# One attention layer and a 64-expert layer on one core: the end of the last chunk laid out anew

## What is computed

```python
# attention: 8 heads of 64 features (d = 512 // 64), softmax(q k / sqrt(8)) v
x = layernorm(x + attention(x) @ Wo + bo)
# shared expert, for every token
shared = (silu(g_s) * y_s) @ w_shared_down          # y_s, g_s = split(x @ w_shared_up)
# routed experts: 64 of them, the 6 best of each token, at most 256 tokens for each
scores = sigmoid(x @ w_gate); w, idx = top_k(scores, 6); w = w / w.sum()
pos = running count of the tokens that chose this expert before   # valid if pos < 256
x_disp[e, pos] = x                                   # dispatch
out = (silu(x_disp @ w_up[gate]) * (x_disp @ w_up[value])) @ w_down   # per expert
x = layernorm(x + ... )   # shared + sum over the 6 of w * out, gathered back
```

## Time and profile before

| | us |
|---|---|
| median of 3 runs (lowest to highest) | 1390.62 (1387.7 to 1397.6) |
| the profiled execution, its own time | 1395.11 |
| its span, first to last instruction | 1393.3 |
| PE busy | 1280.9 (92%) |
| DVE busy | 1017.0 (73%) |
| ACT busy | 901.2 (65%) |
| POOL busy | 664.8 (48%) |
| mean granted clock of TensorE, share of full | 0.974 |

### The profile page before, as it was taken

How to read it: one execution, slowest core, us unless ns; L and a number is a source line. 1 busy time by engine, 2 the same in 40 slices (tenths; PEclk the granted TensorE clock), 3 DMA queues, 4 the chain that set the end, 5 groups by cost and what they waited for, 6 DMA issues and landing times.

```text
span 1393.3 us, 24378 instructions
## 1 busy us (share of the span) xinstructions
PE 1280.9 (92%) x8129; PEld 1068.5 (77%) x8129; DVE 1017.0 (73%) x1879; ACT 901.2 (65%) x1639; POOL 664.8 (48%) x662
## 2 busy tenths in 40 slices
PE   6999799999999999999999999996678999999596
PEld 4888599899899899799799799796456767767332
DVE  4623488789799899799799789796445677677376
ACT  5411398878688688688688688686114666666242
POOL 0002122235636636636636636546363888888511
PEclk9999899999999999999999999998798999999899
DMA  6049966112423424324334333334455999997597
GB/s 232 0 186 353 344 215 217 55 37 86 136 70 129 130 86 137 105 86 137 112 95 129 121 102 127 108 107 140 157 204 171 335 353 346 347 359 274 208 419 303
DMA packets 155754, 252.78 MB, mean 181 GB/s; under 512 B 18660, under 2 KB 98916, under 8 KB 153201
## 3 DMA queue, kind: packets, MB, share of 16 engines
q1 hardware_dynamic: 130144, 192.19, 40.9%
q0 software_dynamic: 20992, 50.38, 9.5%
q10 hardware_dynamic: 4496, 8.65, 1.7%
HBM read 118.95 MB, written 134.33 MB: 182 GB/s over the span
## 4 chain that ended last, share of the span: by engine, by line
PE 66%; issue 12%; DMA 6%; SPq 4%; DVE 4%; POOL 4%; ACT 3%; another core or an unknown queue 2%; POOLq 0%; DVEq 0%; ACTq 0%
PE pv_acc L1256 13%; PE slot L1237 13%; PE slot L1224 12%; PE slot L1119 8%; PE slot L1333 4%; PE slot L1283 4%; PE misc L1170 4%; PE pv_acc L1119 4%; DMA got<-y_hbm 3%; SPq L397 3%; DVE rows_lo L1059 2%; ACT rows_hi L783 2%; PE slot L1355 1%; DMA moved<-scaled 1%
## 5 line engine op out<-in xcount | busy, mean ns | idle before, releaser
L740 ACT ACTIVATE p_hi<-slot 128x512 fp32r<-128x512 f32 x512 | 279.8, 596 | 108.6 <-PE slot L1224 86.4
L590 POOL TENSOR_TENSOR p_lo<-prob,p_hi 128x512 fp32r<-128x512 f32 x128 | 165.1, 1290 | 363.4 <-ACT prob L742 356.9
L1237 PE MATMUL slot<-k_stack,q_stack 128*128 128x512 f32 x1024 | 300.8, 416 | 8.5 <-DMA q_stack<-q_hbm 8.5
L753 ACT ACTIVATE prob<-prob,row_min 128x1024 f32<-128x1024 f32 x256 | 296.4, 1158 | 12.9 <-DVE prob L1035 12.9
L1014 DVE TENSOR_TENSOR p_lo<-slot,p_hi 128x512 fp32r<-128x512 f32 x384 | 251.3, 681 | 37.6 <-ACT p_hi L740 31.0
L1256 PE MATMUL pv_acc<-p_hi,v_pair 128*128 128x256 f32 x1024 | 265.6, 292 | 3.9 <-POOL p_lo L590 3.2
L1224 PE MATMUL slot<-ident,prob 128*128 128x128 f32 x2048 | 265.2, 272 | 1.2 <-ACT prob L753 1.2
L1256 PE MATMUL pv_acc<-p_lo,v_pair 128*128 128x256 f32 x1024 | 255.1, 282 | 0.0
L1224 PEld LDWEIGHTS slot<-ident,prob 128*128 128x128 f32 x2048 | 230.8, 140 | 1.7 <-DVE prob L1035 1.6
L1256 PEld LDWEIGHTS pv_acc<-p_hi,v_pair 128*128 128x128 f32 x1024 | 193.0, 189 | 18.0 <-issue 8.6
L1256 PEld LDWEIGHTS pv_acc<-p_lo,v_pair 128*128 128x128 f32 x1024 | 192.8, 188 | 11.7 <-issue 3.3
(11 more groups left out here) (142 smaller groups left out, 2092.4 us busy)
## 6 DMA issues: line engine op xcount, KB each, us to landing
disp_hbm<-zeros SPq DMA_DIRECT2D x64, 512.0 KB, 5.5
rows<-disp_hbm SPq DMA_DIRECT2D x64, 512.0 KB
y_hbm<-zeros SPq DMA_DIRECT2D x48, 512.0 KB
got<-y_hbm SPq DMA_DIRECT2D x16, 1536.0 KB, 11.9
q_stack<-q_hbm SPq DMA_DIRECT2D x128, 128.0 KB
up_w<-in_L_ffn_w_up SPq DMA_DIRECT2D x64, 256.0 KB
down_w<-in_L_ffn_w_down SPq DMA_DIRECT2D x32, 256.0 KB
q_hbm<-q_hi SPq DMA_DIRECT2D x8, 512.0 KB, 2.6
```

What stands on the lines that cost most here:

```text
L590: e.tensor_tensor(p_lo[1][:, 2:4, :], prob[:, m % 2, :, (4 * u + 2) * P:(4 * u + 4) * P], p_hi[1][:, 2:4, :].bitcast(F32), ALU.subtract).t ...
L740: e.activation(p_hi[b][:, two, :], view[:, two, :], ACT.Copy).then_inc(a_phi, 1)
L753: e.activation(keys, keys, ACT.Exp, bias=row_min[:, me % 2, j, 1:2], scale=-1.0, accum_out=row_sum[:, me % 2, j, half:half + 1]).then_inc( ...
L1237: made = e.matmul(slot[:, n * BANK:(n + 1) * BANK], qs[:, part, j * P:(j + 1) * P], k_stack[:, ms % H, keys], start=part == 0, stop=part == 1)
```

## The change

- **Loads within the last chunk.** The rows of items 0 to 6, the residual tiles of the last chunk, the shared weights and seven `up_w` are loaded by SP during the last chunk, each over the keys of a head that is used up (`head_used` waits for that head's last scores). The last chunk's two tiles live in `rows[7]`, which is also item 7: it is not stored and loaded again. The shared weights are split in the attention's drain.
- **Both tiles side by side.** The last chunk's second tile gets its own bank (`pv_acc`), `x1_t`, scores and so on (`routing_of`, `bank_of`).
- **A hand-laid order.** `last_end` replaces `chunk_end` for the last chunk; it starts in the items' loop, and there are three `side_step`s in an iteration: `after(n, part)` names the place after flip (0), up (1) or down (2) of iteration n.
- `P0`, `P1` become 12, 34. The notes of the second tile of chunk 6 wait until attention is over; the scatters of each tile have their own semaphore. The notes of the last chunk come after all its scatters. The table is turned at n = 9, not 7. Weights of experts 0 to 3 are split at n = 0 to 3, not 4 to 7. SP's loads are in a written order.

```diff
-        AHEAD, CLEAR, SIDE, K_ROUTE = NB - 1, NCH - 1, 4, 16
-        P0, P1 = 14, 38
+        AHEAD, K_ROUTE, END = NB - 1, 16, NCH - 1
+        P0, P1 = 12, 34
+        def head_used(e, h):
+            e.wait_ge(p_scores, (END * H + h) * STEPS + STEPS)
+        def rows_of_chunk(c, j):
+            return rows[NS - 1][:, j, :] if c == END else resid[j][:, :]
+        def routing_of(c, j):
+            return routings[1 if c == END and j else 0]
+        def bank_of(c, j):
+            return pv_acc if c == END and j else misc
+        def after(n, part):
+            return 3 * (n + 2) + part
+        def split_at(n):
+            g = n if n < NU else n + NU - NS if n >= NS else -1
+            return range(g, g + 1) if 0 <= g < E else range(0)
...
# SP, called once in each step with s - END * H * STEPS
+            def load_for_shared(s):
+                if s in (6, 10, 14):
+                    for n in (0, 1):
+                        load_rows(e, (s - 6) // 2 + n)
+                elif s == 19:
+                    for j in range(QT):
+                        load_resid(END, j)
+                elif s == 22:
+                    head_used(e, 4)
+                    e.dma_start(sup_w[:, :, :], w_sup[:, :, :]).then_inc(d_sup, 16)
+                    e.dma_start(sdown_w[:, :], w_sdown).then_inc(d_sup, 16)
+                elif s == 28:
+                    load_rows(e, NS - 2)
+                elif s == 33:
+                    for g in range(NB - 1):
+                        load_up(e, g)
...
# SP, after the steps
-            attention_over(e)
-            load_resid(NCH - 1, 1)
...
+            for pair in range(NB // 2):
+                load_down(e, pair)
+            for g in (NB, NB + 1, NB - 1, NB + 2):
+                load_up(e, g)
+            for n in range(NS, NS + NU):
+                load_rows(e, n)
+            load_up(e, NB + 3)
+            for j in range(2):
+                e.wait_ge(d_tabw[j], 16 * TOPK * NCH)
+            e.dma_start(table[:, :], table_hbm.rearrange("(c p) one -> c (p one)", p=P)).then_inc(d_tab, 16)
...
# POOL
                 for k in range(0, TOPK, 2):
-                    yield from to(P1 + 30 + k)
+                    yield from to(P1 + (30 if c < END - 1 else 64) + k)
                     note_rows(2 * c + 1, k)
                     note_rows(2 * c + 1, k + 1)
+            def last_end(c):
+                to = ticks()
+                yield from to(after(-1, 1))
+                root(c, 0)
+                root(c, 1)
+                yield from to(after(1, 0))
+                count(c, 0)
+                for j in range(2):
+                    yield from to(after(1 + j, 2))
+                    e.wait_ge(v_route[j], K_ROUTE * c + 15)
+                    for k in range(TOPK):
+                        scatter(c, j, k)
+                yield from to(after(4, 0))
+                for j in range(2):
+                    for k in range(TOPK):
+                        note_rows(2 * c + j, k)
...
# ACT
+            def last_end(c):
+                to = ticks()
+                yield from to(after(0, 0))
+                flip_x1(c, 0)
+                yield from to(after(0, 1))
+                raise_score(c, 0)
+                flip_x1(c, 1)
+                yield from to(after(0, 2))
+                raise_score(c, 1)
...
# DVE
+            def last_end(c):
+                to = ticks()
+                yield from to(after(-1, 1))
+                add_resid(c, 0)
+                measure(c, 0)
+                add_resid(c, 1)
+                normalize(c, 0)
+                measure(c, 1)
+                yield from to(after(0, 0))
+                normalize(c, 1)
+                for j in range(2):
+                    yield from to(after(0, 1 + j))
+                    for part in (score_experts, choose, mark, mark_any):
+                        part(c, j)
+                yield from to(after(1, 0))
+                for j in range(2):
+                    for part in (sum_top, share, pick_rank, find_place, find_slots, keep_weights):
+                        part(c, j)
+                    yield from to(after(1, 2))
...
# PE
+            def last_end(c):
+                to = ticks()
+                yield from to(after(-1, 1))
+                out_project(c, 0)
+                out_project(c, 1)
+                yield from to(after(0, 0))
+                turn_x1(c, 0)
+                yield from to(after(0, 1))
+                gate_scores(c, 0)
+                turn_x1(c, 1)
+                yield from to(after(0, 2))
+                gate_scores(c, 1)
+                yield from to(after(1, 0))
+                rank(c, 0)
+                yield from to(after(1, 2))
+                rank(c, 1)
```

More of the change, by code:

```diff
@@ L201, in build @@
         d_qst, d_q = [sem(f"dma_q_store{i}") for i in range(2)], [sem(f"dma_q{i}") for i in range(2)]
-        d_moved, d_feats, d_st, d_scat = (sem(f"dma_{n}") for n in ("moved", "feats", "x1_store", "scatter"))
+        d_moved, d_feats, d_st, d_st_late = (sem(f"dma_{n}") for n in ("moved", "feats", "x1_store", "x1_store_late"))
+        d_scat = [sem(f"dma_scatter{j}") for j in range(2)]
         d_resid = [sem(f"dma_resid{j}") for j in range(QT)]
@@ L455, in sync @@
                 side_step(jobs)
-            attention_over(e)
-            load_resid(NCH - 1, 1)
[L459 to L471, removed]
+            for pair in range(NB // 2):
[8 more added lines that the diff above has]
+            e.dma_start(table[:, :], table_hbm.rearrange("(c p) one -> c (p one)", p=P)).then_inc(d_tab, 16)
+            loaded, ups = NS + NU, NB + NU
+            for n in range(NS - 2, NI):
+                while loaded < NI and loaded <= n + (AHEAD if loaded < NS + NB else NB + 1):
+                    load_rows(e, loaded)
+                    loaded += 1
                 for g in range(ups, min(E, n + 4)):
@@ L636, in gpsimd @@
                                 oob_is_err=False).then_inc(d_y[y], 16)
-                for _ in range(SIDE):
-                    side_step(jobs)
+                side_step(jobs)
             def final_root(t):
@@ new lines, in keep_weights, with route @@
+            def keep_weights(c, j):
+                own = routing_of(c, j)
+                e.scalar_tensor_tensor(out=weight_of[:, 2 * c + j, :], in0=own.place[:, :], scalar=float(CAP),
+                                       in1=own.top[:, 0:TOPK], op0=ALU.is_lt, op1=ALU.mult).then_inc(v_route[j], 1)
+            def route(c, j, clock, start):
+                for n, part in enumerate((score_experts, choose, mark, mark_any, sum_top, share, pick_rank,
+                                          find_place, find_slots)):
+                    yield from clock(start + 6 + 2 * n)
+                    part(c, j)
@@ L1284, in tensor @@
                     made.then_inc(p_flip, 1)
-                for _ in range((3 if n == -2 else 1) * SIDE):
-                    side_step(jobs)
+                side_step(jobs)
                 i = n + 1
```

376 lines of the change are left out of this document (195 added, 181 removed).

## The result

The changed kernel is **slower** by 1.7%: 1418.1 us (median of 4 runs, 1412.9 to 1422.9) against 1393.7 (4 runs, the three of the table above and one more, 1387.7 to 1397.6), ratio 1.0166, 95% interval 1.0138 to 1.0194. The forecast was 1358 us. The profiled execution has a span of 1415.0 us (before 1393.3).

The account below looks back on a forecast made before the run. POOL, never idle from first to last `y_hbm` scatter, was taken as the bound, so its first scatter decides: 110.9 us after attention's old end before, 2.8 + 71.3 + 2 = 76.1 after, gain 34.8; forecast 1358 us, range 1349 to 1377.

Parts of the forecast that it names:

- attention, with P0 and P1 earlier and the loads beside it: Attention up to its end: loads hide under full PE and side jobs keep their order; 0, within 2 us.
- The drain: End of attention: four POOL scatters ahead of the last `p_lo` make PE wait, so attention ends 2.8 us later.
- From A' to the first `y_hbm` scatter: From attention's new end to POOL's first `y_hbm` scatter: 71.3 us, plus 2 for the clock.
- The 110.9 us of the kernel before: From attention's last matmul to POOL's first `y_hbm` scatter in the old kernel: the base for the gain.
- From the first scatter to the end: POOL's first `y_hbm` scatter to its last 235.3 us, then 82.5 us to the end: nothing changed.
- Rival 1: Behind attention: ACT's unexplained waits return in POOL's unbroken run; 1376 us with both, 1363 to 1372 with one; chance 0.25.
- Rival 2: Behind attention: notes and table set the end if DVE routes late; `scat` 8 us late gives 1366; chance 0.06.
- Rival 3: Shared stage behind attention: the clock stays at 1.2 GHz, + 48 us, 1408 us; chance 0.04.
- Rival 4: Last chunk: a load over a used key holds SP's queue; 1361 us, whole failure 1385 to 1395; chance 0.03.
- The 0.03 for "slower": Whole kernel: the chance given to a time above the no-change bound of 1404.5 us.

Follow-up runs that it names:

- e6: The changed kernel run once more, nothing altered: median 1399.8 us, ratio 1.0172 to the kernel before.
- e5: The kernel before run once more, nothing altered: median 1378.9 us.
- e2: The kernel before with only P0, P1 = 12, 34 in place of 14, 38: ratio 1.0273 to the kernel before.
- e1: The changed kernel with P0, P1 put back to 14, 38: 1368.4 us, ratio 0.9934 to the kernel before.
- e4: The changed kernel with P0, P1 = 14, 38 and the last chunk's twelve notes left out: 74.7 us from the last head's `scaled` to the first `y_hbm` scatter.
- e11: The changed kernel with P0, P1 = 14, 38, six row loads at s = 7, 11, 15, last chunk's bias additions at 21 and 23: ratio 0.9845 to 0.9882.

## Why the prediction was wrong, point by point

**The step that failed** is the first one: "attention, with P0 and P1 earlier and the loads beside it: 0, within 2 us". On runs without the long waits the attention ends 45.8 us later (959.9 to 1005.7); 4.5 of them are the drain, which had a term of its own, and 41.3 are this step. I argued that PE is full there, that P1 moves by two whole steps and that the side jobs keep their order against `p_lo`. The first two are true, and neither says what a use of `misc` does to the head's own use. The third looked at the order only: with P1 = 34 PE's wait for `p_lo` at a chunk's first head rose from 0.4 to 1.7 us. A stage with PE at 10.00 of 10 us has no slack either: a wait that is put ahead of a `spread` lengthened its head by as much (1.4 us), in each of seven chunks. By the chunks' own lengths, six cost 33.1 us (e6 against e5, 636.3 and 603.2 us from the end of chunk 0 to that of chunk 6), and e2, with nothing but the two numbers changed, 37.6 in all. The remainder is nearly all in the last chunk. Of the loads, the step said that they hide: they do by their volume, but not by their place in the queue (5.5 to 7.5 us in e1; in e6 the head took 18.1 us against 16.9 to 17.1 in the chunks before it, so about 1 us there).

**The drain**, forecast 2.8 us: PE waited 5.1 us for POOL's `p_lo` against 0.9, and the last head took 13.2 us in e6 against 8.6 in e5, 4.5 more. The mechanism, four scatters ahead of it, was right; it was under-sized by 1.7 us. The sum had POOL at work throughout, but in e6 POOL stood idle for 0.69 us ahead of the join, and the second scatter took 1.82 us in place of 0.97. With P1 = 38 the scatters fall behind it (9.1 us).

**From A' to the first `y_hbm` scatter**, forecast 73.3 with the clock: 73.7 to 74.8 in all later kernels with the new order, and 84.6 in the first execution. Its parts (last scatter 50.0 for 47.1, notes 66.5 for 63.7) were each some 3 us late and mostly hidden. e4 shows the notes hidden.

**What was subtracted from.** The 110.9 us of the kernel before held 15.8 us that no later execution has the earlier trace rows. I took ACT's unexplained waits as a property of the old order, so that the sum counted them as gained by the change. Against e5's 95.1 the gain behind the attention is 20.3 us, not 37.6.

**From the first scatter to the end**, "nothing is changed": span less Y is 318.1 in e5, 316.7 in e6. It held.

**Rival 1** (ACT's waits come back) had its symptom and not its mechanism: they came back in the same set of runs, at 3.65, 7.65 and 6.11 us, and POOL's unbroken run of scatters and notes stands in e1 and e6 without them. Its times (1363 to 1376) missed because they built on the same attention. **Rival 2** fell with e4. **Rival 3**: its place was wrong, its kind of effect small; the clock was 0.76 in the first 15.5 us behind the attention and 1.00 from 1027.5 to 1045.4 (the windows' own numbers), in a stretch of 14.9 busy us of 17.9. **Rival 4** occurred in small: SP sent the seven `up_w` loads (1.75 MB, from 987.10 in e6) ahead of head 62's `moved`, which then landed 3.3 us after its issue (1.86 in the earlier trace rows), and the join behind it was late by POOL's 0.69 us above. None of them ended on the slower side by way of the attention. The 0.03 for "slower" was a statement about the mechanisms I had listed, and the edit that applied to seven chunks out of eight had been given one sentence.

Put together on runs without the long waits: attention + 45.8, behind it - 20.3, rest - 1.5 = + 24.0 us of span (1373.1 to 1397.1). In e11 it is + 7.2, - 20.8, + 0.4 = - 13.2 (1359.9).

## What to carry to other kernels

Where two pieces of work share a bank and the order on the engine is fixed, write down for each place which of the two comes first and who must read before the next may write (here the ranks, 1.4 us in each turn): a shift by one step of the loop can turn "just behind" into "just ahead" in every turn of the loop. An edit in the steady part of a kernel is multiplied by its turns, so cost it before the edits at the end, however small it looks. A transfer that hides by its bytes can still hold up the small one that is issued behind it. And a wait that the profile can't name is not yet a property of the kernel: look whether a second execution has it before you count it as gained.

## What the runs showed of the hardware

The same program took 1393.7 us in the first set of runs and 1377.9 to 1378.9 in the later ones, 1.1% apart, each consistent in itself (1387.7 to 1397.6 and 1373.1 to 1383.2). In the profiled executions of the slower set ScalarE waited 3.65 to 13.41 us for something that the profile doesn't name, until 2 to 17 us after the modelled ends of the matmuls that it reads; in all eleven profiles of the other runs this is absent. What was late, and why, was not settled.

A 64 KB transfer took 8.2 us from its issue to its consumer's start when it was issued behind 1.75 MB of the same engine's transfers of the last 5 us, and 3.1 us when 1 MB of these came behind it. The Trainium skill ("DMA: Bandwidth & Descriptors", Queues, rings and completion order) says that an engine of the DMA turns between rings, a packet from each. All of these transfers come from SP, and the profile shows SP's transfers in one queue, so that the rule gives the small one no turn of its own; that it was late behind the large ones agrees with that.
